# Where the gathers of quads 1 to 3 stand: in two trains ahead of the multiplications, or spread over the steps of the first tile and the groups of layer 1

## The reference

```
e  = stack(tbl_f[ids[:, f]])                      # (512, 39, 16)
X1 = einsum('hjk,bjd,bkd->bhd', W0, X0, X0) + b0  # (512, 128, 16)
X2 = einsum('hjk,bjd,bkd->bhd', W1, X0, X1) + b1
X3 = einsum('hjk,bjd,bkd->bhd', W2, X0, X2) + b2
z  = concat(X1.sum(2), X2.sum(2), X3.sum(2))
h  = relu([z, dense_ctx] @ W_top1 + b_top1)
h  = relu(h @ W_top2 + b_top2)
y  = h @ W_top3                                   # (512, 1)
```

## Time and profile before

| what | value |
|---|---|
| median of 3 runs | 698.75 us (696.44 to 703.89) |
| the profiled execution's own time | 701.35 us |
| its span | 699.5 us |
| mean granted TensorE clock | 0.983 |
| busy share PE / DVE / ACT / POOL | 95% / 73% / 81% / 65% |
| chain that ended last, by engine | PE 90%, ACT 3%, another core or an unknown queue 2%, DVE 2% |

### The profile page before, as it was taken

How to read it: one execution, slowest core, us unless ns; L and a number is a source line. 1 busy time by engine, 2 the same in 40 slices (tenths; PEclk the granted TensorE clock), 3 DMA queues, 4 the chain that set the end, 5 groups by cost and what they waited for, 6 DMA issues and landing times.

```text
span 699.5 us, 10372 instructions
## 1 busy us (share of the span) xinstructions
PE 666.5 (95%) x2686; PEld 492.0 (70%) x2686; DVE 507.4 (73%) x977; ACT 566.5 (81%) x1997; POOL 454.9 (65%) x445
## 2 busy tenths in 40 slices
PE   4297889999999999999999999999999999999998
PEld 4275657777777777777777777777777777776683
DVE  5266667787777777877777788777777787888690
ACT  3266578889888888988888888898988888999672
POOL 7728547877787777788787877787887736432000
PEclk9789999999999999999999999999999999999999
DMA  6023241323433323233231313131213122004300
GB/s 205 14 64 98 37 96 34 96 37 96 97 95 81 108 25 110 35 90 71 73 88 6 96 7 95 8 94 8 95 6 97 5 84 85 2 1 148 145 1 0
DMA packets 107532, 46.02 MB, mean 66 GB/s; under 512 B 80897, under 2 KB 92941, under 8 KB 107474
## 3 DMA queue, kind: packets, MB, share of 16 engines
q1 hardware_dynamic: 101427, 42.82, 23.1%
q0 software_dynamic: 5120, 1.29, 2.2%
q10 hardware_dynamic: 927, 1.26, 0.6%
HBM read 13.81 MB, written 5.24 MB: 27 GB/s over the span
## 4 chain that ended last, share of the span: by engine, by line
PE 90%; ACT 3%; another core or an unknown queue 2%; DVE 2%; DMA 1%; issue 1%; POOL 0%; SPq 0%; ACTq 0%; DVEq 0%
PE ps_y L913 21%; PE ps_y L915 20%; PE ps_y L914 20%; PE ps_x L841 13%; PE ps_g L930 5%; PE ps_tr L810 2%; ACT prod L556 2%; PE ps_y L974 1%; PE ps_y L975 1%; PE ps_y L976 1%; PE ps_y L988 1%; PE ps_y L924 1%; PE ps_tr L818 1%; DMA g_all<-in_L_rec_W 1%
## 5 line engine op out<-in xcount | busy, mean ns | idle before, releaser
L556 ACT ACTIVATE prod<-ps_y,xt 128x128 f32<-128x128 f32 x1792 | 492.8, 440 | 81.7 <-PE ps_y L915 69.1
L913 PE MATMUL ps_y<-w_hi,x_hi 128*128 128x512 f32 (+1 forms) x640 | 313.5, 490 | 7.8 <-ACT prod L556 5.6
L915 PE MATMUL ps_y<-w_hi,x_lo 128*128 128x512 f32 (+1 forms) x640 | 249.9, 390 | 0.0
L914 PE MATMUL ps_y<-w_lo,x_hi 128*128 128x512 f32 (+1 forms) x640 | 249.8, 390 | 0.0
L417 POOL TENSOR_TENSOR prod<-prod 128x512 f32<-128x512 f32 x120 | 154.8, 1290 | 113.9 <-ACT prod L556 106.4
L737 DVE SCALAR_TENSOR_TENSOR prod<-ps_y,xt,prod 128x128 f32<-128x128 f32 x576 | 164.4, 344 | 52.5 <-PE ps_y L915 44.6
L388 POOL DMA_INDIRECT rows<-in_table,index x160 | 156.3, 977 | 39.2 <-issue 32.6
L913 PEld LDWEIGHTS ps_y<-w_hi,x_hi 128*128 128x128 f32 x640 | 121.2, 189 | 65.6 <-issue 21.1
L744 DVE TENSOR_REDUCE prod<-prod 128x128 f32<-128x1536 f32 (+1 forms) x64 | 116.3, 1817 | 63.5 <-ACT prod L556 63.5
L914 PEld LDWEIGHTS ps_y<-w_lo,x_hi 128*128 128x128 f32 x640 | 121.3, 190 | 47.6 <-issue 24.2
L412 POOL TENSOR_TENSOR room<-room 117x512 f32<-117x512 f32 (+1 forms) x105 | 134.9, 1289 | 19.7 <-DMA room<-room 19.6
(11 more groups left out here) (118 smaller groups left out, 327.0 us busy)
## 6 DMA issues: line engine op xcount, KB each, us to landing
room<-room SPq DMA_DIRECT2D x75, 234.0 KB
room<-room SPq DMA_DIRECT2D x45, 78.0 KB
emb_room<-rows SPq DMA_DIRECT2D x168, 5.0 KB
rows<-in_table,index POOLq DMA_INDIRECT x160
w_hi_dram<-g_all SPq DMA_DIRECT2D x5, 512.0 KB
w_lo_dram<-g_all SPq DMA_DIRECT2D x5, 512.0 KB
room<-room SPq DMA_DIRECT2D x15, 156.0 KB
g_all<-in_L_rec_W SPq DMA_DIRECT2D x9, 256.0 KB, 5.8
```

Source lines behind the costliest of these rows:

```text
L556: ins = nc.scalar.activation(prod[:, SLOT[k] + m // 2, :, m % 2], ps_y[:, g % YBANKS, m * H:(m + 1) * H], ACT.Copy, scale=xt[:, q % 2, ti, ...
L913: nc.tensor.matmul(y, hi, w1_hi[:, cols], start=True, stop=False)
L914: nc.tensor.matmul(y, hi, w1_lo[:, cols], start=False, stop=False)
L915: nc.tensor.matmul(y, lo, w1_hi[:, cols], start=False, stop=True).then_inc(y_made, 1)
```

## The change

The ten gathers of quad 1 no longer follow quad 0's at once: two do, and each of the other eight waits on POOL for a step of the first tile's way. Quad 2's gathers wait for numbers of finished groups (`THIRD_GATHERED_AT`, against `y_made`); its last three stand between the multiplications of quad 1. Of quad 3's, four follow directly, then comes `repeat_rows(2)`, then six that wait for groups of T3. Quad 4's index and first six gathers come ahead of quad 2's multiplications, which are now all in the list before the loop; then four gathers, `repeat_rows(3)` and the first two multiplications of quad 3. POOL's loop of additions begins at T8 in place of T4 (`FREE_QUADS` = 2), and DVE's `reduce_early` sums ten pairs up to T7. Quad 1 has the late table for layer0 (`SECOND_SUMMED_AFTER`) too. Quad 2's rows are turned at (0, 7) of quad 1 (T4) in place of (2, 9) of quad 0 (T2), and copied there; quad 3's at (3, 2) and (3, 6) of quad 1 (T7) in place of (2, 4) and (2, 6) (T6). W2's turns, loads and saves are one quad or three tiles later.

```diff
@@ -65,19 +65,25 @@
 
 
 
+
 MULTIPLIED_IN = {(0, 0): [2], (0, 1): [3], (1, 0): [4], (1, 1): [5], (2, 0): [6]}
 MULTIPLIED_AHEAD = {(3, 1): [0, 1]}
 GATHERED_IN = {(0, 1): range(0, 2), (1, 1): range(2, 4), (2, 1): range(4, 8), (3, 0): range(8, 9),
                (3, 1): range(9, GATHERS)}
 REPEATED_IN = (1, 1)
 TURNED_AFTER, KEPT_AFTER = (2, 4), (2, 6)
-THIRD_TURNED_AFTER, THIRD_KEPT_AFTER = (2, 9), (3, 0)
+FREE_QUADS = 2
+THIRD_TURNED_AFTER, THIRD_KEPT_AFTER = (3, 2), (3, 6)
 SUMMED_AFTER = {(0, 2): 0, (0, 5): 1, (0, 8): 2, (1, 1): 3, (1, 8): 4, (2, 8): 5, (3, 2): 6}
 SECOND_SUMMED_AFTER = {(1, 9): 0, (2, 1): 1, (2, 3): 2, (2, 5): 3, (2, 7): 4, (3, 0): 5, (3, 2): 6}
 
 FIRST_SUMMED_AFTER = {2: [0], 3: [1], 4: [2], 5: [3], 6: [4], 7: [5, 6]}
 
-SECOND_REGROUPED_AFTER, SECOND_TURNED_AFTER, SECOND_KEPT_AFTER = 3, 7, 7
+SECOND_REGROUPED_AFTER = 3
+NEXT_TURNED_AFTER, NEXT_KEPT_AFTER = (0, 7), (0, 7)
+
+THIRD_GATHERED_AT = [0, 8, 9, 11, 13, 15, 17]
+FOURTH_GATHERED_AT = [0, 0, 0, 0, 30, 32, 34, 36, 38, 39]
 SUM_D_AFTER = 6
 
 
@@ -92,7 +98,7 @@
 W2_SIZE = 4
 W2_GROUPS = -(-F // W2_SIZE)
 W2_PARTS = W2_GROUPS // 2
-W2_TURNED_IN = {QT * (n // 2 + 1 + n % 2) + (0 if n % 2 else 3): n for n in range(W2_GROUPS)}
+W2_TURNED_IN = {QT * (n // 2 + 2) + (3 if n % 2 else 0): n for n in range(W2_GROUPS)}
 W2_TURNED_AFTER = 4
 W2_SAVED_BEHIND = 4
 
@@ -339,10 +345,10 @@
                     cut_window(q, c, cut[q % 2])
                 if q + 1 < QUADS:
                     lay_out(q + 1)
-                if q <= W2_PARTS:
-                    if q == 1:
+                if 0 <= q - 2 < W2_PARTS:
+                    if q == 2:
                         sp.wait_ge(prep_tr, len(TURNS))
-                    load_w2(q - 1)
+                    load_w2(q - 2)
                 if 0 <= q - W2_SAVED_BEHIND < W2_PARTS:
                     save_w2(q - W2_SAVED_BEHIND)
                 if q == 2:
@@ -422,10 +428,29 @@
             nc.gpsimd.affine_select(out=ident[:], in_=ident[:], compare_op=ALU.not_equal, fill=1.0, base=0,
                                     pattern=[[-1, P]], channel_multiplier=1).then_inc(ident_made, 1)
             pool.wait_ge(ids_ld, 32)
-            for q in range(2):
-                make_index(q)
-                for g in range(GATHERS):
-                    gather(q, g)
+            make_index(0)
+            for g in range(GATHERS):
+                gather(0, g)
+
+            make_index(1)
+            gather(1, 0)
+            gather(1, 1)
+            pool.wait_ge(regrouped_dve, 1)
+            gather(1, 2)
+            pool.wait_ge(emb_made, 1)
+            gather(1, 3)
+            pool.wait_ge(first_x0, 1)
+            gather(1, 4)
+            pool.wait_ge(first_xa, 1)
+            gather(1, 5)
+            pool.wait_ge(first_z, 2)
+            gather(1, 6)
+            pool.wait_ge(first_z, 4)
+            gather(1, 7)
+            pool.wait_ge(first_summed, 1)
+            gather(1, 8)
+            pool.wait_ge(first_x1_lo, 1)
+            gather(1, 9)
 
             pool.wait_ge(gathered[1], 16 * GATHERS)
             pool.wait_ge(emb_turned, 1)
@@ -434,18 +459,29 @@
             ins.then_inc(regrouped_pool, 1)
             repeat_rows(1)
             make_index(2)
-            for g in range(GATHERS):
+            for g, made in enumerate(THIRD_GATHERED_AT):
+                wait(pool, y_made, made)
                 gather(2, g)
             for c in range(CHUNKS):
                 multiply(1, c)
+                if len(THIRD_GATHERED_AT) + c < GATHERS:
+                    gather(2, len(THIRD_GATHERED_AT) + c)
             make_index(3)
-            for g in range(4):
+            for g, made in enumerate(FOURTH_GATHERED_AT):
+                if g == 4:
+                    repeat_rows(2)
+                wait(pool, y_made, made)
                 gather(3, g)
-            repeat_rows(2)
-            for g in range(4, GATHERS):
-                gather(3, g)
+            make_index(4)
+            for g in range(6):
+                gather(4, g)
+            for c in range(CHUNKS):
+                multiply(2, c)
+            for g in range(6, GATHERS):
+                gather(4, g)
+            repeat_rows(3)
             for c in MULTIPLIED_AHEAD[3, 1]:
-                multiply(2, c)
+                multiply(3, c)
 
             def between(q, ti, part):
                 if q + 1 < QUADS:
@@ -462,7 +498,7 @@
                     for g in GATHERED_IN.get((ti, part), ()):
                         gather(q + 3, g)
 
-            for T in range(QT, TILES):
+            for T in range(FREE_QUADS * QT, TILES):
                 for part in range(2):
                     add_groups(T, part)
                     between(T // QT, T % QT, part)
@@ -581,9 +617,9 @@
                         for f in range(FPG // 2):
                             ins = regroup(nc.scalar.copy, 1, f)
                         ins.then_inc(regrouped_act, 1)
-                    if (T, g) == (0, SECOND_KEPT_AFTER):
-                        keep_x0(1)
-                    if q + 2 < QUADS and (ti, g) == (KEPT_AFTER if q > 0 else THIRD_KEPT_AFTER):
+                    if q < FREE_QUADS and (ti, g) == NEXT_KEPT_AFTER:
+                        keep_x0(q + 1)
+                    if FREE_QUADS - 1 <= q < QUADS - 2 and (ti, g) == (KEPT_AFTER if q >= FREE_QUADS else THIRD_KEPT_AFTER):
                         keep_x0(q + 2)
                     if g == 7 and T > 0:
                         keep_g(T - 1)
@@ -739,9 +775,9 @@
 
             def reduce_early(T):
                 dve.wait_ge(act_step, ACT_STEPS * T + 5)
-                wait(dve, pool_step, len(ADDED) * (T + 1 - QT))
+                wait(dve, pool_step, len(ADDED) * (T + 1 - FREE_QUADS * QT))
                 wait(dve, reduced, REDUCTIONS * T)
-                nc.vector.tensor_reduce(prod[:, BIASED, :, 0], prod[:, EARLY if T >= QT else EARLY_FIRST].rearrange("p n h l -> p h n l"), AX_XY,
+                nc.vector.tensor_reduce(prod[:, BIASED, :, 0], prod[:, EARLY if T >= FREE_QUADS * QT else EARLY_FIRST].rearrange("p n h l -> p h n l"), AX_XY,
                                         ALU.add).then_inc(reduced, 1)
 
             def reduce_late(T):
@@ -824,7 +860,7 @@
                 if n % 2 == 0:
                     pe.wait_ge(w2_ld[n // 2], 16 if n // 2 < W2_PARTS - 1 else 32)
 
-                pe.wait_ge(x0_made, T // QT + 3 if n % 2 == 0 else T // QT + 2)
+                pe.wait_ge(x0_made, T // QT + (2 if T % QT == 0 else 3))
                 wait(pe, w2_lo_made, n)
                 src = w2_home(True, n)
                 for m in range(min(W2_SIZE, F - W2_SIZE * n)):
@@ -949,11 +985,11 @@
                     if T == 0:
                         for c in FIRST_SUMMED_AFTER.get(g, ()):
                             sum_rest(c)
-                    if (T, g) == (0, SECOND_TURNED_AFTER):
-                        turn_rows(1)
-                    if q + 2 < QUADS and (ti, g) == (TURNED_AFTER if q > 0 else THIRD_TURNED_AFTER):
+                    if q < FREE_QUADS and (ti, g) == NEXT_TURNED_AFTER:
+                        turn_rows(q + 1)
+                    if FREE_QUADS - 1 <= q < QUADS - 2 and (ti, g) == (TURNED_AFTER if q >= FREE_QUADS else THIRD_TURNED_AFTER):
                         turn_rows(q + 2)
-                    order = SUMMED_AFTER if q > 0 else SECOND_SUMMED_AFTER
+                    order = SUMMED_AFTER if q >= FREE_QUADS else SECOND_SUMMED_AFTER
                     if nxt and (ti, g) in order:
                         layer0(q + 1, order[ti, g])
 
```

## The result

| | median | runs |
|---|---|---|
| before | 699.47 us | 20 |
| changed | 703.85 us | 20 |

The ratio is 1.0057, 95% interval 1.0037 to 1.0077: 0.6% slower, clear of noise, inside the range of 688 to 707, and on the other side of the 0.2% faster that was forecast. The profiled executions, 701.35 and 702.46 us, understate it: before's is 1.9 over its median, the changed one's 1.4 under.

What follows compares the result with a forecast made beforehand. PE, 95% busy, was taken as the bound, with idle time before 132 us blamed on long gather trains. Terms -5.0, -7.9, +2.2, +9.1 and +0.4 sum to -1.2 us: 700.1 profiled, 697.5 as median; range 688 to 707.

Steps and rivals of the forecast that it cites:

- The start: Before T0: spreading quad 1's gathers between the first tile's steps removes stops; 5.0 us gained, bounds 0 to 6.3.
- The slow rival: First 90 us: stops not caused by gather trains come again; +9.9 us, 708.6 in all; chance 0.2.
- T0 to T3: Quad 2's gathers spread: waits for ACT, slow clock and a turn go; 52.1 us shrinks to 44.2, 7.9 gained.
- T4 to T7: Quad 1's new plan: 40.4 us becomes 37.6 plus 5.0 of losses, a term of +2.2.
- The train: Beside T4 and T5: twelve gathers in a row cause stops, within a loss taken as 5 us (2.4 to about 8).
- The products: T4 to T7: quad 2's first two products end at 61.4 and 64.8, wanted at 60.0 and 63.7; 2.4 us lost.
- part 4: Hand-over to T8: late copies make PE wait 2.7 and 4.2 us, plus 2.2 of slow clock; +9.1 us.
- part 3: Quad 1's plan, T4 to T7: base 37.6 us plus 5 of losses against 40.4; +2.2 us.
- The reductions: T4 to T7: ten-pair reduce_early adds about 1 us of VectorE work per tile, covered beside PE's work.
- T8: Quad 3's first products come 4.8 and 12.0 us in; waits 6.9 us plus slow clock 2.2, 9.1 in all.
- threshold of about 9 us: Before T4: the result ends on the slow side once less than about 9 us come back there.
- part 1: Quad 1's gathers spread between the first tile's steps: 5.0 us gained; 0 if the SBUF rule explains the stops.

Runs made afterwards that it cites:

- e4: The kernel before with only the eight waits between quad 1's gathers; 693.12 us, ratio to before 0.993.
- e7b: The changed kernel with half the rows left out in the long train's twelve gathers, third job; 703.76 us, ratio to before 1.0064.
- e10b: The changed kernel with a short GpSimd addition ahead of eleven of the long train's twelve gathers, third job; 699.49 us, ratio to before 1.001.
- a3: The changed kernel, unchanged, run again in the fourth job, without stops; 691.33 us, ratio to before 1.0119.
- e1: The changed kernel with quad 4's first six gathers split: four behind multiply(2,0), the rest later behind repeat_rows(3); 698.71 us, ratio to before 1.0008.
- a2: The changed kernel, unchanged, run again in the third job, with stops; 705.23 us, ratio to before 1.0073.
- e6: The kernel of e1 with six GpSimd additions of 1.29 us where the changed kernel has quad 4's gathers; ratio to before 1.0109.
- e6b: The kernel of e6 run again in the fourth job, without stops; ratio to before 1.0104.
- e7: The changed kernel with half the rows in the long train's twelve gathers, second job, without stops; ratio to before 1.0106.
- e5: The changed kernel with quad 2's ten gathers in one train again, fourth job, without stops; ratio to before 1.0091.
- b2: The kernel before, unchanged, run again in the third job, with stops; 700.36 us.

## Why the prediction was wrong

**The start: right.** T0 was forecast near 33.8 and begins at 33.3; -5.0 taken, -5.5 measured. Both stops behind 24 us are gone. That stops are due to the gathers was argued from a correlation there; e4 shows that spreading them is enough, and e7b and e10b that what counts is how many follow at that pace, not their rows. The slow rival (the stops come again, nothing is gained) fell.

**T0 to T3: right.** 43.4 against 44.2 forecast, no wait of PE for ACT in it.

**T4 to T7: the step that failed.** The term was +2.2 us, with 5 for its losses over a base of 37.6, and measured were 8.8, with losses of 11.6. The mechanisms were for the most part the ones named: twelve gathers in a row, late results, then waits for quad 2's products. The sizes were off.

*The train* was left 2.6 of the 5; it cost 5.9 (changed kernel 49.2, a3 and e1 43.3). The old trains cost 5.6 of waits and 1.9 of slow clock for two; the longest of all was taken at less than one of them.

*The products* were priced at 2.4 us of waits and no more, in two waits. The wait was that, in one, for the product behind the windows (2.3 in e1, 2.4 in a3), but PE's clock falls behind it, which part 4 of the prediction had charged at T8 and part 3 had not. The timeline of PE and the windows of a3:

```profile
76.58 0.50 PE L949 MATMUL ps_y<-w_hi,x_hi 128*128 128x512 f32 x1 [1.14 <-DVE prod L773]
...
95.57 1.12 PE L877 MATMUL ps_x<-room,w0t 117*128 117x512 f32 x2 [2.42 <-POOL room L418]
98.85 1.72 PE L877 MATMUL ps_x<-room,w0t 117*128 117x512 f32 x2
```

```profile
85.00:93.00 8.00, 8.00 (x36) 5.78 (x35) 7.04 (x13) 7.43 (x29) 3.27 (x4) 1.00 0.67 192
93.00:101.00 8.00, 5.58 (x14) 3.45 (x14) 4.48 (x8) 2.92 (x11) 6.75 (x6) 0.79 0.26 12
```

A mean clock of 0.79 over 8 us is 1.7 us of work lost.

*The reductions.* PE also waited 1.14 us for DVE in T4, for the ten-pair `reduce_early` that the prediction had covered by a mean over the span (394.6 of 508 us busy). No chunk of layer0 lies in T4, so PE comes back for the next bank sooner, and the mean said nothing about the cover there.

5.9 + 2.4 + 1.7 + 1.1 = 11.1 of the 11.6; 0.5 is not assigned.

**T8: the waits right, the slow clock wrong.** 9.1 taken, 7.2 measured (7.1 in a3, 9.1 in a2). The products were to be there 4.8 and 12.0 us behind T8's start, and were at 5.5 and 12.5 (130.16 + 1.27 and 137.19 + 1.28, less 125.97). PE waits 3.34 us for the first (2.7 forecast) and then runs at half speed, 2.05 us for a chunk that takes 1.10 in e10b below:

```profile
131.57 2.05 PE L877 MATMUL ps_x<-room,w0t 117*128 117x512 f32 x2 [3.34 <-POOL room L418]
...
138.53 1.13 PE L877 MATMUL ps_x<-room,w0t 117*128 117x512 f32 x2 [0.50 <-POOL room L418]
```

The second wait was forecast at 4.2 and shows 0.50: at half the clock PE was itself late. In e10b the same first wait left the clock alone; its timeline and window of PE:

```profile
128.92 1.10 PE L887 MATMUL ps_x<-room,w0t 117*128 117x512 f32 x2 [3.33 <-POOL room L418]
...
135.54 1.12 PE L887 MATMUL ps_x<-room,w0t 117*128 117x512 f32 x2 [2.97 <-POOL room L418]
```

```profile
128.00:138.00 10.00, 6.11 (x24) 4.03 (x25) 2.78 (x9) 2.88 (x12) 4.55 (x5) 1.00 0.51 122
```

Two waits of 3.3 and 3.0, no slow clock, and T8 to T11 takes 44.5, where the changed kernel, with a mean clock of 0.53 from 131 to 138 us, between its waits, takes 44.8 (e6, e6b and e7 are as e10b: 44.5, 44.4 and 44.7). So the arrival of the second product sets the stage: 6.9 us over the 37.6, which is what the forecast had for the two waits alone, and the 2.2 for slow clock came on top of time that the second wait held anyway. Only in a2 does the clock fall behind the second wait, where nothing hides it:

```profile
140.00:146.00 6.00, 6.00 (x18) 4.21 (x17) 2.41 (x4) 3.07 (x10) 5.69 (x6) 0.72 0.22 8
```

That is 1.7 us of work lost, and a2's stage is 2.0 us longer than a3's.

**The sum and the chances.** With 11.6 in place of 5 the sum would have been +5.4 us, and the medians differ by 4.4. The forecast stood at -1.2, so near zero that one term's size set the sign. The text said so only of the gain before T4, with a threshold of about 9 us where its own terms (2.2, 9.1 and 0.4) make 11.7; of the term that failed it did not. The rival on the slow side had its sign from another cause (no gain at the start) and its price from T8, which did decide, with the long train beside it. The rule weighed in part 1 (the Trainium skill, SBUF — State Buffer, "SBUF: two separate sides": PE and ACT wait for nobody at SBUF's ports) does not speak of what was measured: PE's results were held up to 6 us behind gathers in e7b and not behind the same ones paced in e10b. No run here shows whether SBUF has a part in it.

## What to carry to other kernels

Removing a stop at one place and building the same pattern, longer, at another gives the gain back: list every train that the new order makes and price each by its length, from the one that was measured. Do not charge slow clock behind a wait of TensorE by a fixed rule: behind waits of 3.3 us the clock fell to half in the changed kernel and stayed full in e10b, behind 2.4 us it fell in a3 (1.7 us lost), behind 1.6 us it stayed full in e5. Give it a range, and give it nothing where another wait follows that ends at a fixed time, since slow work only fills that wait. And look at how much of a gain exists in all conditions: here the stops that the change removes were missing in half of the jobs, and the waits for copies that it adds were in all.

## What the runs showed of the hardware

Gathers issued by GpSimd at one per 1.2 to 1.25 us, ten or twelve in a row, held back TensorE's results in the first comparison and in two later jobs: ScalarE waited for them 4.2 us (e4), 4.6 (changed kernel), 6.0 (a2) and 6.8 (b2) at a stretch. Trains of four and of six in e1 did not. In three other jobs the same trains held back nothing, and the kernel before took 683 us in place of 699. Half the rows per gather changed nothing (5.86 us against 5.94), a pace of one per 1.9 us ended it. While its results were late TensorE's own matmuls went on until it needed an answer: in the changed kernel ScalarE stood still from 86.33, TensorE from 88.43.

The clock granted behind a wait was not the same in like places: with a wait of 3.3 us at the same chunk of T8, the lower level, 1.2 GHz, came in the changed kernel (0.53 from 131 to 138 us) and not in e10b (1.00 from 128 to 138), and the stage took 44.8 and 44.5 us.

Medians of the same kernel in different jobs on the same kind of chip differed by 2.5% (683.0 to 700.4 us), several times the interval of a ratio taken within one job.
